# Moving residual and tile additions from VectorE to TensorE and ScalarE inside a selective-scan loop

## The reference, cut to what matters

```python
h = einsum('btc,oc->bto', x, W_base) + b_base + 2 * lora(x, cond)      # L0_cond
y_f = mamba(h)                      # in_proj, causal conv, silu, selective scan
y_r = flip(mamba(flip(h)))          # the same in the other direction
x1 = x + (y_f + y_r) @ out_proj.T   # both gated by silu(z)
X2 = einsum('bnt,bot->bno', x1, w_bot) + bias       # L0_cond2
logits = X2 @ Wg + bg;  topv, topi = top_k(logits, 2);  w = softmax(topv)
out = x1 + X2 + sum over the two chosen experts of FFN(w * X2)
```

## Time and profile before

| | |
|---|---|
| median of three runs | 1405.6 us (1405.03 to 1408.69) |
| the profiled execution | 1403.74 us, its span 1401.9 us |
| PE busy | 1299.0 us, 93% of the span |
| DVE busy | 944.0 us, 67% |
| POOL busy | 970.1 us, 69% |
| ACT busy | 714.6 us, 51% |
| the loop's twelve tile steps and six output blocks | between about 445 and 925 us |

### The profile page before, as it was taken

One profiled execution on the slowest core, in us unless ns is written; L12 is line 12 of the kernel. 1 busy time (PEld: TensorE's weight loads), 2 busy tenths in 40 slices (PEclk: granted clock), 3 DMA queues, 4 the chain that ended last, 5 costly groups with the idle time before them and its releaser, 6 DMA issues. The chain is left out here.

```text
span 1401.9 us, 16597 instructions
## 1 busy us (share of the span) xinstructions
PE 1299.0 (93%) x5300; PEld 779.8 (56%) x5300; DVE 944.0 (67%) x1154; ACT 714.6 (51%) x1262; POOL 970.1 (69%) x508
## 2 busy tenths in 40 slices
PE   8999989999998889899797888899999999999997
PEld 4333333344333334333343333457999999999996
DVE  3998999999999999999999999964111111111110
ACT  4887776687786577776767564411111111111111
POOL 1998999999999999999999999834222222222211
PEclk9999999999999999999999999999999999999999
DMA  5554554554556464555456554608898898888882
GB/s 201 185 165 150 167 165 154 173 183 155 165 178 182 139 202 149 175 165 176 158 180 182 185 173 144 191 5 327 304 316 313 316 319 320 311 313 322 312 319 45
DMA packets 105497, 290.33 MB, mean 207 GB/s; under 512 B 9649, under 2 KB 19506, under 8 KB 89922
## 3 DMA queue, kind: packets, MB, share of 16 engines
q1 hardware_dynamic: 95762, 271.17, 55.7%
q0 software_dynamic: 9648, 18.09, 6.4%
HBM read 271.41 MB, written 9.96 MB: 201 GB/s over the span
## 5 line engine op out<-in xcount | busy, mean ns | idle before, releaser
L434 PE MATMUL ps_y<-arena,ident 128*128 128x512 f32 x1024 | 500.7, 621 | 56.3 <-POOL arena L1178 55.9
L1178 POOL TENSOR_TENSOR arena<-arena 128x1024 f32<-128x1024 f32 x192 | 457.6, 2402 | 19.8 <-DVE arena L916 14.4
L434 PEld LDWEIGHTS ps_y<-arena,ident 128*128 128x128 f32 x1024 | 192.7, 196 | 325.2 <-issue 217.0
L1162 POOL TENSOR_TENSOR arena<-arena 128x1024 f32<-128x1024 f32 x127 | 303.9, 2393 | 6.1 <-issue 4.5
L717 ACT ACTIVATE ps_de<-arena,An 128x512 f32<-128x512 f32 x256 | 176.2, 688 | 227.4 <-DVE arena L913 226.7
L1229 POOL DMA_INDIRECT out_x<-arena x39 | 61.8, 1584 | 317.5 <-ACT arena L851 300.3
L897 DVE TENSOR_TENSOR ps_u<-ps_du,arena 128x512 f32<-128x512 f32 x256 | 178.6, 698 | 23.9 <-DVE arena L927 8.6
L1129 DVE TENSOR_TENSOR arena<-ps_du,arena 128x512 f32<-128x512 f32 x39 | 27.0, 691 | 232.2 <-PE ps_du L597 232.2
L717 ACT ACTIVATE arena<-arena,An 128x512 f32<-128x512 f32 x256 | 181.1, 707 | 0.0
L913 DVE TENSOR_TENSOR_SCAN arena<-ps_de,hlast,arena 128x512 f32<-128x512 f32 x128 | 163.0, 1274 | 0.8 <-ACT arena L717 0.8
L913 DVE TENSOR_TENSOR_SCAN arena<-ps_de,arena 128x512 f32<-128x512 f32 x128 | 155.3, 1213 | 4.0 <-ACT arena L717 4.0
(11 more groups left out here) (221 smaller groups left out, 1485.1 us busy)
## 6 DMA issues: line engine op xcount, KB each, us to landing
arena<-bc_scratch SPq DMA_DIRECT2D x256, 512.0 KB, 4.7
arena<-in_W SPq DMA_DIRECT2D x117, 1024.0 KB, 7.0
arena<-arena POOLq DMA_DIRECT2D x15, 512.0 KB, 4.9
arena<-in_xT SPq DMA_DIRECT2D x2, 1024.0 KB, 5.7
arena<-in_w2c SPq DMA_DIRECT2D x1, 2048.0 KB, 8.6
arena<-in_xT SPq DMA_DIRECT2D x4, 512.0 KB, 6.2
X_scratch<-stg SPq DMA_DIRECT2D x12, 128.0 KB, 4.8
out_x<-stg SPq DMA_DIRECT2D x12, 128.0 KB, 5.0
```

The costliest lines, as they stand in the source:

```text
L434: t = e.matmul(Y[j][:, :], ident[:, :], hc[:, i % NP, j, :], start=False, stop=(n == 15))
L1162: e.tensor_tensor(uA[:, turn % 2, :, :], duA.rearrange("p (o t) -> p o t", o=1).to_broadcast([128, 2, TH]), ring[:, turn % NR, 0, :, :], A ...
L1178: e.tensor_tensor(hc[:, i % NP, :, :], hh[:, i % NH, :, :], c, ALU.mult).then_inc(gp_hc, 1)
```

## The change

Inside the loop the two additions of DVE are gone. For an output block PE adds the residual as a fifth matmul, identity times `X[b]`, into the same sum (it now waits for the load of x itself), and ACT copies the finished sum to `X[b]`, in its step `i + 3`. For a tile PE computes X2 twice, once into each half of the bank, and adds the transpose of x1 to the second as an ordinary accumulating matmul by the identity; ACT copies all 512 columns at once to `sX` and `sB`. The semaphore `ac_X` goes: `tile_T` and the stores wait for `freed` of the bank. The output blocks (1, 0, mo) and the last four tiles stay as they were.

```diff
@@ PE: out_block
-                                 start=(k == 0), stop=(k == 3))
+                                 start=(k == 0), stop=(k == 3 and (b, h) == (1, 0)))
+                if ks[-1] == 3 and (b, h) != (1, 0):
+                    e.wait_ge(l_x, 16 * XT_NO[b, h])
+                    t = e.matmul(PS[p][:, :], ident[:, :], X[b][:, mo, HB[h]], start=False, stop=True)
@@ PE: tile
+            def x2_and_sum(b, cols, p):
+                for o in (0, C):
+                    for k in range(2):
+                        e.matmul(PS[p][:, o:o + C], X[b][:, k, cols], wbot[:, b, k, :], start=(k == 0), stop=False)
+                    t = e.matmul(PS[p][:, o:o + C], ones_r, bias2, start=False, stop=(o == 0))
+                for k in range(2):
+                    t = e.matmul(PS[p][:, C + k * 128:C + k * 128 + 128], X[b][:, k, cols], ident[:, :], start=False,
+                                 stop=(k == 1))
+                t.then_inc(full[p], 1)
-                for k in range(2):
-                    e.matmul(PS[p][:, 0:C], X[b][:, k, cols], wbot[:, b, k, :], start=(k == 0), stop=False)
-                e.matmul(PS[p][:, 0:C], ones_r, bias2, start=False, stop=True)
-                for k in range(2):
-                    t = e.transpose(PS[p][:, C + k * 128:C + k * 128 + 128], X[b][:, k, cols], ident[:, :])
-                t.then_inc(full[p], 1)
+                x2_and_sum(b, cols, p)
@@ PE: tile_T
-                e.wait_ge(ac_X, TILE_NO[b, i] + 1)
+                is_free(("x2", b, i))
@@ ACT
-                e.activation(sX, PS[p][:, 0:C], ACT.Copy).then_inc(ac_X, 1)
+                e.activation(stg[:, st, 0:2, :].rearrange("p w c -> p (w c)"), PS[p][:, :], ACT.Copy).then_inc(freed[p], 1)
+            def out_block(b, h, mo):
+                p = is_full(e, ("o", b, h, mo))
+                e.activation(X[b][:, mo, HB[h]], PS[p][:, :], ACT.Copy).then_inc(freed[p], 1)
...
+                if i - 3 in OUT_AT:
+                    out_block(*OUT_AT[i - 3])
@@ DVE
-                e.tensor_tensor(sB, PS[p][:, C:2 * C], sX, ALU.add).then_inc(freed[p], 1)
...
-                if i - 2 in OUT_AT:
-                    out_block(*OUT_AT[i - 2])
-                if i - 2 in TILE_AT:
-                    tile(*TILE_AT[i - 2])
@@ SP: store
-                e.wait_ge(ac_X, TILE_NO[b, i] + 1)
+                is_read(e, ("x2", b, i))
                 e.dma_start(X_dram[tt * 128:tt * 128 + 128, :], sX).then_inc(l_st[st], 16)
-                is_read(e, ("x2", b, i))
```

More of the change, by code:

```diff
@@ L218, in build @@
         ac_z = sem("z")
-        ac_X, ac_XT, pe_lg, dv_mx, dv_lg, gp_sB = (sem(n) for n in ("X", "XT", "lg", "mx", "lgt", "gsB"))
+        ac_XT, pe_lg, dv_mx, dv_lg, gp_sB = (sem(n) for n in ("XT", "lg", "mx", "lgt", "gsB"))
         dv_rt, ac_ex, pe_rx, gp_rw, pe_inv = (sem(n) for n in ("rt", "ex", "rx", "rw", "inv"))
@@ L943, in out_block @@
                 e.tensor_tensor(X[b][:, mo, HB[h]], PS[p][:, :], X[b][:, mo, HB[h]], ALU.add).then_inc(freed[p], 1)
-            def tile(b, i):
-                st, sX, sB, sT = tile_buffers(b, i)
-                p = place["x2", b, i][0]
-                e.wait_ge(ac_X, TILE_NO[b, i] + 1)
-                if st < 2 and TILE_NO[b, i] >= 2:
-                    e.wait_ge(l_st[st], 32 * (TILE_NO[b, i] // 2))
-                e.tensor_tensor(sB, PS[p][:, C:2 * C], sX, ALU.add).then_inc(freed[p], 1)
             def tile_top(b, i):
```

## The result

The changed kernel takes 1408.76 us, median of 21 runs (1403.35 to 1413.78); before, 1405.1 us in 21 runs (1402.08 to 1408.83). The ratio is 1.0024 with a 95% interval of 1.0014 to 1.0034: slower by 2 to 5 us. The forecast was 1405.3 us, 0.3 us under before and within the noise. Its sign was wrong: the time lies in the wide range (1399 to 1411 us) and just outside the forecast's own (1402.5 to 1408.5). The profiled execution of the changed kernel, 1403.35 us (span 1401.5), was the quickest of its 21: the profile shows places, and not the whole of the loss.

A forecast was written before the change was run, and what follows sets the result against it. DVE was taken to set the pace, with ACT or PE holding it at a few places. Terms -2.4 - 1.3 + 0.7 + 3.2 - 0.5 = -0.3 us gave 1405.3 us on the median's scale; range 1402.5 to 1408.5, wide 1399 to 1411.

The forecast's parts named there:

- rival (c): In the loop, POOL, as busy as DVE, holds the pace: DVE gains -1 in place of -3.7, 1408.0 us; chance 0.08.
- Output blocks on DVE, -2.4 us: Six additions leave DVE's output-block steps, each shortening its step by 0.40 us of its 667 ns: -2.4 us.
- Tile additions and ACT's copies, -1.3 + 0.7 us: Nine of twelve tile additions save DVE 0.14 us each; ACT's longer copy costs 0.22 in three places.
- PE's price of a tile, 1.6 us: PE's growth per tile from second X2, 1.3 to 1.4 us, and identity matmuls; bounds 1.3 and 2.2 us.
- (d): In tiles, identity matmuls cost four times a transpose, about 1.1 us for two: +1.2 us, 1406.5 us; chance 0.04.
- "so about 0" at tile (0, 4): Logits end at 661.67, DVE comes at 663.17: 1.5 us of room, so PE's longer tile costs about 0.
- 0 for the sums: In output-block steps nobody waits for PE's sums: 0, or 1.7 us at the upper end.
- rival (b): Longer X2 makes PE the bound among tiles: +5.0 us, 1410.6; sign: logits waits at four or more tiles; chance 0.17.
- Tile (0, 1): 1.6 foreseen: Logits end at 768.17 and DVE starts at 768.22, having waited 0.17 us: no room, so +1.6 us.
- (0, 6): 1.6 foreseen: DVE's maxima already wait 1.29 us for this tile's logits, so PE's longer tile adds +1.6 us.
- rival (a): PE keeps up without clock falls near 700 and 867 us: -3.8 or -5.4 us, 1400.2 to 1401.8; chance 0.24.
- Clock, -0.5 us: Longer tile (1, 4) fills PE's idle time ahead of 867 us; the second clock fall may vanish, half of 1.1 us counted.

The follow-up runs named there:

- no_sum: Kernel before with ACT copying all 512 columns and DVE's twelve tile additions left out, PE's work as before; 1406.37 us, ratio 1.0008 to before.
- x2_twice: Kernel before with X2 of the twelve loop tiles computed twice into the same columns on PE, all else as before; 1409.59 us, ratio 1.0037 to before.
- before_b: Kernel before, unchanged, profiled once more in one execution; steps 189 to 196 took 26.07 us, against 26.53 in its first profile.
- tile_only: Tile half of the change alone against the kernel before, output blocks still added by DVE; 1408.61 us, ratio 1.0036.
- out_only: Output-block half of the change alone against the kernel before, tiles as before; 1400.96 us, ratio 0.9974.

## Why the prediction was wrong

- **What bounds the loop: right.** DVE sets the pace and PE or ACT holds it in places; POOL's rival (c) shows nowhere, the waits of DVE name no product of POOL's. But the list of DVE's waits was read short: it leaves out 1.9 us in two places for PE's sums (L927), most of it 1.76 us at step 227.
- **Output blocks on DVE, -2.4 us: right.** Two blocks shorten steps 141 to 149 by 0.79 us, in every kernel that has the edit, 0.40 each. Alone the half brings 3.7 us by the ratio (interval 1.5 to 5.9).
- **Tile additions and ACT's copies, -1.3 + 0.7 us: right within the noise.** 0.26 us for two additions at 212 to 220, 0.13 each; `no_sum`, which has both, is at 1.0008, so their sum isn't told from 0.
- **PE's price of a tile, 1.6 us: too small.** It is 1.9 to 2.0, inside its bounds. The second X2 costs 1.69 and not 1.3 to 1.4. The one-row bias matmul takes 0.62 us (764.90 to 765.52), where one of the two 256-column matmuls ahead of it takes 0.48 to 0.53; the earlier trace rows had it already, 766.46 to 767.08. The identity matmuls cost 0.55, as the row of 128-column matmuls said, not the 1.1 of the rule that I weighed; (d) falls.
- **Who waits, "so about 0" at tile (0, 4) and 0 for the sums: the step that failed.** I compared only the logits with DVE's arrival. The prediction put nothing on the sums behind a tile. Steps 176 to 184 are longer by 2.0 us, and 2.4 in two further profiles (the clock fell to 0.50 there before and in these two, and not in the first), because the last sums of a unit, their copying by ACT and the next sums stand behind that tile; `x2_twice`, with PE's work alone, has +1.9 there. For the logits of (0, 4) the 1.5 us of room nearly sufficed: DVE waits 0.20 us (661.13). This is rival (b) with its mechanism at another place than its text gave. Its condition, 1.5 us per tile, was met by the prediction's own estimate of 1.6. Its sign, waits for the logits at four places, was met as well, but two of the four are of 0.2 us.
- **Tile (0, 1): 1.6 foreseen, 2.2 measured; (0, 6): 1.6 foreseen, 0.7 to 0.8 measured** against the first profile before, 1.1 to 1.3 against `before_b`. At (0, 6) the low clock ran for 7 us in both profiles before (699.4 to 706.2 in the first) and for 3 us in all three after, which is what rival (a) had foreseen in part; where it lasted 7 us with the tile's longer work (`tile_only`), the stretch is 2.2 us longer.
- **Clock, -0.5 us: the fall did shrink, but not for the reason given.** Steps 239 to 243 take 15.0 to 15.5 us after and 16.4 before; that is -0.9 to -1.4, and more than I gave it. Every kernel with a fall of 7 us there takes 16.1 to 16.4, every one with a shorter fall or none 15.0 to 15.5. The longer tile (1, 4) isn't what decides: `out_only` hasn't got it and takes 15.15, `x2_twice` has its longer X2 and takes 16.08. What does is not shown.

The places read in the profiles add up to less than the ratio's 3.4 us: the two tile stretches of 2.0 and 2.2 and the one of 0.7 are nearly paid by -2.2 (output blocks), -1.2 (tile additions) and -0.9 (steps 239 to 243), which leaves some +0.6 us. The halves, 0.9974 and 1.0036, multiply to 1.0010; with their intervals combined (0.9989 to 1.0031) that agrees with 1.0024. The loop as a whole took 880.2 and 882.9 us in the two profiles before and 879.9, 882.3 and 881.7 in the three after: these five executions show the price at its places, and not the loss of the whole, for which only the 21 executions of each kernel speak. Whether the rest lies in clock falls in untouched steps, which a kernel with other timing meets more or less often, stays open.

## What to carry to other kernels

Price an addition on the busy engine by the distance between its neighbours with and without it: 667 ns busy were 0.40 us of step, 401 ns were 0.13. Where the other engine is called idle, ask what stands behind the new work in its order and who waits for that, not only for the result of the same tile, but for the last sum of a unit, whose reader frees the bank for the next. And put the result that somebody waits for ahead of work that nobody waits for yet: that one swap was worth 4.8 us here (at least 2.0), where the whole change had cost 3.4. It pays only if the next thing behind the same work isn't waited for as well.

## What the runs showed of the hardware

Over the 21 runs of the changed kernel the time goes with the mean granted clock of TensorE: 0.976 with 1413.8 us and 0.986 with 1403.4, correlation -0.83. Yet lifting the clock with filler to 0.99 in the loop did not make it faster. Where a fall lies in the loop matters: a fall of 3 us from step 160 on cost at most 0.7 us of the stretch, one of 14 us 4.8. A matmul with one row (1x256) occupies PE 0.62 us in a chain of float32 matmuls, where one of 128 rows and the same columns takes 0.48 to 0.53: few rows don't make it cheaper.
